# L0 cross-attention: the keys' reciprocal norms go through a row in DRAM, and the step is laid out anew

## The reference

```python
xn = layernorm(x, ln_x_g, ln_x_b)            # context, 8 x 1601 x 256
ln = layernorm(latents, ln_l_g, ln_l_b)      # 8 x 64 x 256
q = (ln @ Wq)                                # split in 16 heads of 64
kv = jnp.concatenate([xn @ Wkv, ln @ Wkv], axis=1)
qn = rmsnorm(q, qn_g) * scale                # x / (norm of the head's 64 values / 8)
kn = rmsnorm(k, kn_g)
sim = jnp.einsum('bhid,bhjd->bhij', qn, kn)  # masked
attn = jax.nn.softmax(sim, axis=-1)
out = jnp.einsum('bhij,bhjd->bhid', attn, v)
return out @ Wout + bout
```

## Time and profile before

| | |
|---|---|
| timed runs | 3336.15 us (3332.85 to 3337.33) |
| the profiled execution | 3327.6 us, of which the span from the first to the last instruction is 3325.8 us |
| mean granted TensorE clock | 0.938 of full speed |
| PE busy over the span | 2892.9 us (87%) |
| DVE, ACT, POOL busy | 1606.0 (48%), 1071.9 (32%), 508.3 us (15%) |
| mix of this layer, line 1339, PE | 437.6 us in 1792 records |
| keys, line 1273, PE | 388.1 us in 1024 records |
| spread, line 1287, PE | 64.4 us in 512 records |
| keys_normed, line 998, DVE | 125.4 us in 128 instructions |
| HBM read and written | 201.99 and 10.58 MB |

### The profile page before, as it was taken

The page is one execution under the profiler, slowest core; times in us unless marked ns, Lnnn a source line. Parts: engine busy times, 40 slices in busy tenths (PEclk is TensorE's granted clock), DMA queues, the critical chain, the costliest instruction groups (busy, mean ns, idle before and its releaser), DMA issues. The chain is left out here.

```text
span 3325.8 us, 44201 instructions
## 1 busy us (share of the span) xinstructions
PE 2892.9 (87%) x17968; PEld 1930.7 (58%) x17968; DVE 1606.0 (48%) x3626; ACT 1071.9 (32%) x1925; POOL 508.3 (15%) x280
## 2 busy tenths in 40 slices
PE   4899999999999999779999978998965789688776
PEld 2465656666665666445555635666942459577644
DVE  4445454545555443535555546764531340355564
ACT  2232323333333322114445536532321423111121
POOL 2011120202020200000000004761010130243200
PEclk8899999999999999889999989998987889899898
DMA  4000000000000000121010001115857149423001
GB/s 135 0 1 22 1 23 6 18 23 1 23 1 23 1 1 1 71 106 41 21 41 21 1 6 33 45 41 203 320 195 229 50 163 324 146 86 113 32 1 32
DMA packets 80704, 215.92 MB, mean 65 GB/s; under 512 B 5232, under 2 KB 53896, under 8 KB 73848
## 3 DMA queue, kind: packets, MB, share of 16 engines
q1 hardware_dynamic: 77528, 204.98, 18.2%
q0 software_dynamic: 2976, 8.13, 0.7%
HBM read 201.99 MB, written 10.58 MB: 64 GB/s over the span
## 5 line engine op out<-in xcount | busy, mean ns | idle before, releaser
L1339 PE MATMUL L_xattn_bank<-L_xattn_keys_tok,L_xattn_probsT 119*128 119x257 f32 (+1 forms) x1792 | 437.6, 389 | 1.4 <-ACT L_xattn_probsT L1172 1.4
L1273 PE MATMUL L_xattn_wide<-L_xattn_keys_feat,weights_a 128*128 128x512 f32 (+2 forms) x1024 | 388.1, 523 | 3.0 <-DVE L_xattn_max L1008 1.3
L1339 PEld LDWEIGHTS L_xattn_bank<-L_xattn_keys_tok,L_xattn_probsT 119*128 119x128 f32 (+1 forms) x1792 | 324.3, 189 | 112.3 <-ACT L_xattn_probsT L1172 42.6
L1166 ACT ACTIVATE L_xattn_scores<-L_xattn_scores,L_xattn_neg_max 128x833 f32<-128x833 f32 x128 | 119.7, 983 | 627.7 <-DVE L_xattn_neg_max L1013 627.7
L1273 PEld LDWEIGHTS L_xattn_wide<-L_xattn_keys_feat,weights_a 128*128 128x128 f32 x1024 | 190.6, 192 | 157.7 <-issue 128.7
L2280 DVE TENSOR_TENSOR_SCAN L_attn_state<-L_attn_decay,L_attn_banks 128x1024 f32<-128x1024 f32 x80 | 182.7, 2286 | 69.6 <-PE L_attn_banks L2483 61.6
L998 DVE TENSOR_TENSOR L_xattn_k_normed<-L_xattn_wide,L_xattn_k_normed 128x834 f32<-128x834 f32 x128 | 125.4, 1021 | 172.8 <-PE L_xattn_wide L1287 172.8
L1555 DVE CUSTOM_DVE_ANT_0 L_xattn_scores<-L_xattn_banks,L_xattn_mask 128x512 f32<-128x512 f32 (+1 forms) x256 | 131.5, 570 | 151.8 <-issue 151.8
L1093 POOL TENSOR_TENSOR L_xattn_keys_tok<-L_xattn_keys_tok,weights_a 119x1792 f32<-119x1792 f32 (+2 forms) x24 | 61.1, 2545 | 938.4 <-DVE L_xattn_keys_tok L933 938.4
L2386 POOL TENSOR_TENSOR L_attn_state<-L_attn_state,L_attn_C_rows 128x1024 f32<-128x1024 f32 x80 | 188.7, 2360 | 70.3 <-DVE L_attn_state L2280 70.2
L1008 DVE CUSTOM_DVE_ANT_0 L_xattn_scores<-L_xattn_wide,L_xattn_mask_row 128x833 f32<-128x833 f32 x128 | 126.4, 1021 | 129.4 <-issue 129.4
(11 more groups left out here) (506 smaller groups left out, 4590.8 us busy)
## 6 DMA issues: line engine op xcount, KB each, us to landing
L_xattn_ctx_feat<-in_ctx_feat SPq DMA_DIRECT2D x24, 1601.0 KB, 10.2
L_ffn_expert_w<-in_x_L_ffn SPq DMA_DIRECT2D x16, 2056.0 KB, 8.4
L_ffn_expert_w<-in_x_L_ffn SPq DMA_DIRECT2D x15, 1028.0 KB, 6.0
L_ffn_expert_w<-in_x_L_ffn SPq DMA_DIRECT2D x15, 1024.0 KB, 5.6
L_xattn_keys_tok<-in_ctx_tok SPq DMA_DIRECT2D x8, 1547.0 KB
L_attn_C_rows<-L_attn_c_rows SPq DMA_DIRECT2D x48, 256.0 KB, 3.2
L_xattn_ctx_tok<-in_ctx_tok SPq DMA_DIRECT2D x8, 1536.0 KB
L_xattn_ctx_tok_and_one<-in_ctx_tok SPq DMA_DIRECT2D x8, 1536.0 KB
```

The source lines that it names most:

```text
L1273: last = nc.tensor.matmul(wide[:, 2 * h + c, 0:n], wk[:, k, p * P:(p + 1) * P], xnT[b % 2][:, k, a:a + n], start=(k == 0), stop=(k == KT - 1))
L1339: last = nc.tensor.matmul(bS[:, 0:D + 1], pT[0:r, c, a, :, :].rearrange("p h q -> p (h q)"), xn[b % 2][0:r, t, :], start=(t == 0), stop=(t ...
```

## The change

Four things are changed, all in `l0_xattn`.

- *The scales.* `spread` and its four products are gone. After Exp, ACT issues two DMAs that store the two heads' rows of `rk` (4 partitions of 417 each) as one row of 1668 in DRAM, `k_scale_rows`, in two buffers. SP waits for them, and for the multiply of the step before, and issues two DMAs that read a row 64 times, onto 64 partitions each of `spread` (`k_scale`) in SBUF. `keys_normed` multiplies by that tile.
- *The order.* `keys_normed(s)` is no longer done in the turn before, but in turn s, between `weights_turned` and `key_clamp(s + 1)`. `scores(s)` wait for it and for the clamp. `swap_max`, `shift` and `exponentials` of step s are done in turn s, behind the scores, and no longer at the beginning of turn s + 1. `turn_weights` is split around the second half of the keys. `mix` takes the tiles in another order, first those that ACT has copied.
- *The loads.* SP's list is one loop over the steps. The context load of 119 rows is cut into one DMA of 112 and one of 7 rows; the loads of batch b + 1 stand behind the scales of step p = 1.
- *The start.* `keys(1)` waits for the first clamp, no longer for the scaled keys of step 0.

The diff, cut to its core (the loops of PE, DVE and ACT are given as rows below it):

```diff
@@ sync
-                for b in range(B):
+                def load_ctx(b):
                     if b >= 2:
                         sp.wait_ge(mixed, NQ * (b - 1))
...
-                    sp.dma_start(xn[b % 2][0:TR, 0:TILES - 1, 0:D], rows[0:near, :].rearrange("(t p) d -> p t d", p=TR)
-                                 ).then_inc(ctx_loaded[b % 2], 16)
+                    far = rows[0:near, :].rearrange("(t p) d -> p t d", p=TR)
+                    for a, c in ((0, EVEN), (EVEN, TR)):
+                        sp.dma_start(xn[b % 2][a:c, 0:TILES - 1, 0:D], far[a:c]).then_inc(ctx_loaded[b % 2], 16)
...
+                def spread_scale(s):
+                    sp.wait_ge(k_scale_stored, 32 * (s + 1))
+                    if s >= 1:
+                        sp.wait_ge(kn_ready, 2 * s)
+                    for h in range(2):
+                        sp.dma_start(spread[h * DH:(h + 1) * DH, :, :].rearrange("p j n -> p (j n)"),
+                                     k_scale_rows[s % 2, h:h + 1, :].broadcast_to([DH, KP])).then_inc(k_scale_moved, 16)
+                load_ctx(0)
+                load_mask(0)
+                sp.wait_ge(latents_ready, 1)
+                for b in range(2):
+                    move_latents(b)
+                load_ctx(1)
+                load_mask(1)
+                for s in range(STEPS):
+                    b, p = divmod(s, NQ)
+                    spread_scale(s)
+                    if p == 1 and 1 <= b < B - 1:
+                        load_ctx(b + 1)
+                        move_latents(b + 1)
+                        load_mask(b + 1)
@@ vector
                 def keys_normed(s):
-                    dve.wait_ge(k_spread, s + 1)
+                    dve.wait_ge(k_scale_moved, 32 * (s + 1))
...
-                        nc.vector.tensor_tensor(k, wide[:, 2 * x:2 * x + 2, 0:QK], k, ALU.mult).then_inc(kn_ready, 1)
+                        nc.vector.tensor_tensor(k, spread[:, 2 * x:2 * x + 2, :], k, ALU.mult).then_inc(kn_ready, 1)
@@ scalar, in key_rnorm
+                    act.wait_ge(k_rnorm, 2 * s + 2)
+                    if s >= 2:
+                        act.wait_ge(k_scale_moved, 32 * (s - 1))
+                    for h in range(2):
+                        nc.scalar.dma_start(k_scale_rows[s % 2, h].rearrange("(j n) -> j n", n=QK), rk[h:P:32, :]
+                                            ).then_inc(k_scale_stored, 16)
@@ tensor, in keys
-                    if s == 1:
-                        pe.wait_ge(kn_ready, h + 1)
-                    elif s:
+                    if s == 1 and h == 0:
+                        pe.wait_ge(k_clamped, 1)
+                    if s >= 2:
                         pe.wait_ge(s_taken, 2 * (s - 2) + h + 1)
@@ tensor
-                def spread(s):
-                    pe.wait_ge(k_rnorm, 2 * s + 2)
-                    for j in range(4):
-                        last = nc.tensor.matmul(wide[:, j, 0:QK], L.const[32 * j:32 * (j + 1), C_SPREAD:C_SPREAD + P],
-                                                rk[32 * j:32 * (j + 1), :], start=True, stop=True)
-                    last.then_inc(k_spread, 1)
...
                 def scores(s):
                     b, p = divmod(s, NQ)
-                    pe.wait_ge(kn_ready, 2 * min(s + 1, STEPS - 1) + 2)
-                    if s + 1 == STEPS:
+                    pe.wait_ge(kn_ready, 2 * s + 2)
+                    if s + 1 < STEPS:
+                        pe.wait_ge(k_clamped, s + 2)
+                    else:
                         pe.wait_ge(s_taken, 2 * s)
...
```

More of the change, by code:

```diff
@@ L776, in l0_xattn @@
     TR, HALF_T = 119, 7
+    EVEN = 112
     TILES = 2 * HALF_T
@@ L786, in l0_xattn @@
     GROUPS = [(0, 0, 4), (0, 4, 3), (1, 0, 4), (1, 4, 3)]
+    MIX_ORDER = [(c, a) for part in (range(4), range(4, HALF_T)) for c in range(2) for a in part]
     CTX_PIECES = [(0, HALF_T), (HALF_T, TILES)]
@@ L811, in l0_xattn @@
         rk = sb("k_rnorm", [P, QK])
+        spread = sb("k_scale", [P, 4, QK])
+        k_scale_rows = nc.dram_tensor(name + "k_scale_rows", (2, 2, KP), F32, kind="Internal").ap()
         sc2 = sb("scores", [P, 2, HALF - TR + P])
@@ L1064, in _ @@
                         score_max(s)
-                        if turns:
-                            keys_turned(b + 1, p - 5, 1)
-                        if b + 1 < B:
-                            if p == 1:
-                                ctx_stats(b + 1, 0)
-                            if p == 2:
-                                ctx_stats(b + 1, 1)
-                                ctx_norm(b + 1, 0)
-                            if p == 3:
-                                ctx_norm(b + 1, 1)
+                    if s >= 2:
+                        keep_result(s - 2)
+                    if s < STEPS:
+                        shift(s)
+                    if turns:
+                        keys_turned(b + 1, p - 5, 1)
+                    if s < STEPS and b + 1 < B:
+                        if p == 1:
+                            ctx_stats(b + 1, 0)
+                        if p == 2:
+                            ctx_stats(b + 1, 1)
+                            ctx_norm(b + 1, 0)
+                        if p == 3:
+                            ctx_norm(b + 1, 1)
                     if behind:
@@ L1210, in _ @@
                         keys_turned(b + 1, p - 5, 1)
+                    if s < STEPS:
+                        exponentials(s)
             @block.tensor
@@ L1366, in _ @@
                 means(0)
-                spread(0)
                 for s in range(STEPS + 2):
@@ L1384, in _ @@
                     if behind:
-                        turn_weights(s - 1, 2)
-                        turn_weights(s - 1, 3)
+                        mix(s - 1, range(4))
                     if ahead:
                         means(s + 1)
-                    if behind:
-                        mix(s - 1, range(5))
-                    if ahead:
-                        spread(s + 1)
-                    if s >= 2:
-                        apply_v(s - 2)
                     if turns:
@@ L1398, in _ @@
                     if behind:
-                        mix(s - 1, range(5, 10))
+                        mix(s - 1, range(4, 6))
                     if s < STEPS:
                         scores(s)
+                    if s >= 2:
+                        apply_v(s - 2)
                     if turns:
@@ L1405, in _ @@
                     if behind:
-                        mix(s - 1, range(10, TILES))
+                        mix(s - 1, range(6, 11))
+                    if s < STEPS:
+                        swap_max(s)
+                    if behind:
+                        mix(s - 1, range(11, TILES))
                 pe.wait_ge(att_ready, STEPS)
```

52 lines of the change are left out of this document (26 added, 26 removed).

## The result

| | median us (lowest to highest) | ratio to before (95% interval) |
|---|---|---|
| before | 3334.5 (3332.3 to 3337.3, 4 runs) | |
| after | 3242.9 (3241.3 to 3248.1, 4 runs) | 0.9728 (0.9711 to 0.9744) |

The forecast was 3257 (3238 to 3290), faster: 91.6 us came out where 79 were forecast. The profiled execution took 3242.2 us, its span is 3240.4, 85.4 shorter than before. All of that lies between the start and the last scores: the first scores start at 100.72 for 112.53, 11.8 us, and the 63 steps behind them take 1122.7 for 1196.3 us, 73.6. What follows is as long as before.

What follows compares the result with a forecast made beforehand. PE was taken as the bound, the only full engine. Steps 63, context load 8 and ramp 8 us sum to 79, taken from the median 3336.15: 3257 us, 2.4% faster, range 3238 to 3290.

Steps and rivals of the forecast that it cites:

- The steps: Cross-attention steps on PE: each 1.02 us shorter, taken as 1.0 over 63 steps, 63 us.
- the start: Everything up to the first steps: 8 us from the cut context load and 8 us from the ramp.
- the extra 0.64 us: Mean step over plain step, from the next batch's keys and statistics: 0.64 us a step, taken as unchanged.
- Spread, 0.92 a step: Spread's four products on PE: removing them takes 0.92 us out of each of 64 steps.
- The plain step, 17.34: One plain step on PE, key product to key product: 16.91 us plus a 0.43 wait, 17.34 for 18.36.
- D: Rival: the shift, now ahead of DVE's statistics and norms, saves 16 us more; 3241 us, chance 0.10.
- A: Rival: DVE's multiply, both factors in SBUF, clashes with POOL's passes at p = 3 and 4; 30 us, 3287, chance 0.14.
- The prediction's own sign of being wrong: DVE's multiplies in p = 3 taking over 2 us would show the clash with POOL.
- B: Rival: the means, clamp, scores chain is 0.4 us longer, breaking the cover below 0.1; 25 us, 3282, chance 0.11.
- C: Rival: late scale broadcasts make a ring of 6.0 + L a step (L: landing); 3423 us at L = 14, chance 0.05.
- The load, 8: First context load, cut into 112 and 7 rows: lands near 29 us, 8 us earlier, bounds 0 and 8.
- The ramp, 8: First steps: keys of step 1 wait only for the first clamp; gain 8 us, between 4 and 10.

Runs made afterwards that it cites:

- e4: e1 with DVE's shift put back behind the next batch's statistics and norms, as before the change; 3239.3 us.
- e1: The kernel after, with POOL's gain and bias passes for the next batch held until DVE's multiply at p = 3 (second piece: p = 4) is done; 3220.3 us.
- e11: The kernel before, with POOL's passes held back until they lie over DVE's multiply, which has one operand in PSUM; 3331.3 us, ratio 1.0000.
- e2: The kernel after, with each context load again one transfer of 119 rows; 3247.1 us.
- e8: The kernel after, DRAM round trip kept, but the keys' multiply put back a step earlier, straight behind their clamp; 3952.1 us.
- e5: The kernel after, with two further broadcasts into an unread tile ahead of each step's two, the multiply waiting for all four; 3258.5 us.
- e3: The kernel after, with four products of spread's shape, never read, put ahead of the scores in every step but the last; 3309.6 us.
- e9: The kernel after, with four further broadcasts into unread tiles ahead of each step's two, the multiply waiting for all six; 3426.8 us.

## Why the prediction was right, and where not

The sum was 79 and 91.6 came out. The steps gave 73.6 for 63, the start 11.8 for 16, and the scatter of the runs 6.2: before's profiled execution lies 6.9 us below its median of 3334.5, after's 0.7 below its own. The mechanism of the steps was right. That the sum held as well as it did is in part luck, as the points on the extra 0.64 us and on the start say.

- *Spread, 0.92 a step:* right; put back, it costs 0.91.
- *The plain step, 17.34:* 17.24. The hand-over of ACT's copy to the first mix was put at 0.15 us and is 0.05 (copy ends 385.52, mix 385.57), so the gain is 1.12 a step and not 1.0, 70.6 us in 63 steps where 63 were taken. The other 3 us of the trace's 73.6 are the shorter last step, the extras of the next point, and slow clocks that one trace has and the other has not. The sum hid how much ACT's order held up: 1.41 us a step.
- *The extra 0.64 us a step, "I leave them as they are":* the step of the argument that failed, though not its sum. Per batch the extras were 5.52 and are 5.30. Inside, two changes cancel: the shift's new place is worth 19.1 us (e4 against e1; D was put at 16) and the clash costs 22.6 (e1; A was put at 30), of which 18.3 are the longer steps 2-3. They were written down as rivals of each other; they were both true, and it was luck that they weigh the same. The prediction's own sign of being wrong, multiplies over 2 us in p = 3, came true while its time held. Against A stood that all old multiplies kept to 1.02 us; e11 shows why that told nothing: their first operand was in PSUM.
- *A's size:* p = 3 costs 2.6 a batch for 3.2 (a figure that the prediction's own times, 12.5 and 8.8, do not give: they differ by 3.7); p = 4 nothing for 1, since there 0.8 us more on DVE falls into the cover.
- *B:* the cover held, by 0.18 us where less than 0.1 was laid out.
- *C:* the landing, 6.9 by estimate, is 5.1, and there is room for twice the bytes in a plain step.
- *The load, 8:* 7.1 (e2 against e1); the statistics start near 30 and not 29.
- *The ramp, 8:* from the first clamp to the keys of step 2 before took 26.6 us (90.28 to 116.89) and after takes 18.8 (87.41 to 106.19): 7.8. This is read from the traces; no run puts the old start back. The chain was not quite the one laid out: at a clock of 1.00 (e1) the first scale's round trip bounds it and the keys of step 1 do not, and it is as long, 18.9.
- *Both together:* 15.9 to the first scores by e1's trace, but 11.8 in the profiled run of after, where the clock over the first keys and what stands ahead of them took most of the difference. The keys of step 2 start at 106.19 there and not near 101.

Not undone by any run, and so not told apart: the split of the turns around the second half of the keys, and the new place of the swap of the maxima.

## What to carry to other kernels

When an operand moves from PSUM to SBUF, look up what GpSimd does at that moment: the pair of multiplies is as fast alone and takes nearly three times as long beside a GpSimd pass (5.49 us for 1.96), and a wait that starts the passes 5.7 us later, behind the multiply, costs nothing. The round trip through DRAM was free only with its reader a step later (11.1 us a step in e8 otherwise), so moving the reader is the change, and the reader's order has to be followed on every engine that feeds it. Rivals with different places should be added up, not chosen between.

## What the runs showed of the hardware

- A DVE multiply of 128 x 834 with both operands in SBUF takes 1.02 us alone and up to 4.53 beside a POOL pass of 119 x 1792, which itself goes from 3.73 to 4.38 (after). With one operand in PSUM neither changes (e11).
- The granted clock behind a wait of PE: 0.50 to 0.52 over the next 3.1 us after each of 63 waits of 8.2 to 10.1 us (e8; 0.869 over the kernel for 0.938). Over the 4.4 us behind waits of 2.5 us at one and the same place: 1.00 seven times in e2, 1.00 six times and 0.50 once in after, 0.61 to 0.67 five times of seven in e5, 0.50 to 0.67 seven times in e3. What decides between these stays open. Once in after it cost 2.84 us.
- Broadcasts of a DRAM row to 64 partitions, 417 KB each: the two that count land 5.1 us after their issue by themselves (after), 8.0 with two more ahead of them (e5), 10.8 with four more (e9), where the multiply starts 14.1 us behind the first issue.
